# A selective scan on one core: rows of B and C transposed two chunks ahead, y from states over 32 rows, D times x inside the first two products

## What is computed

```python
    dA = jnp.exp(dt[:, :, None, :] * A[None, :, :, None])
    dB = dt[:, :, None, :] * Bt
    def step(h, inp):
        dA_t, dB_t, x_t, C_t = inp
        h = dA_t[:, :, None, :] * h + dB_t[:, :, None, :] * x_t[..., None]
        y_t = jnp.einsum('bhds,bhs->bhd', h, C_t)
        return (h, y_t)
    ...
    return jnp.moveaxis(ys, 0, -1) + D[None, :, None, None] * x
```

## Time and profile before

| | us |
|---|---|
| median of three runs | 1005.8 |
| the profiled execution | 1010.08 |
| its span, first to last instruction | 1008.3 |

### The profile page before, as it was taken

The page is one execution under the profiler, slowest core; times in us unless marked ns, Lnnn a source line. Parts: engine busy times, 40 slices in busy tenths (PEclk is TensorE's granted clock), DMA queues, the critical chain, the costliest instruction groups (busy, mean ns, idle before and its releaser), DMA issues.

```text
span 1008.3 us, 15638 instructions
## 1 busy us (share of the span) xinstructions
PE 916.3 (91%) x4658; PEld 714.5 (71%) x4658; DVE 747.3 (74%) x2003; ACT 534.5 (53%) x1037; POOL 487.7 (48%) x549
## 2 busy tenths in 40 slices
PE   3999899999776787777799999999999999999997
PEld 3887788887454555445678777787777777787776
DVE  5677778564776778666778787788778787788875
ACT  2767677776987998776433332333333332333330
POOL 2145577887788788886544413344034431340000
PEclk8889899999788989778899999999999999999999
DMA  5227765547447444632531401413104131040001
GB/s 171 84 85 215 193 157 171 145 79 234 134 118 171 131 130 124 183 106 86 188 127 43 167 23 39 146 42 144 43 21 166 39 120 70 21 166 21 21 1 42
DMA packets 63690, 110.07 MB, mean 109 GB/s; under 512 B 18539, under 2 KB 44437, under 8 KB 60565
## 3 DMA queue, kind: packets, MB, share of 16 engines
q1 hardware_dynamic: 54388, 90.23, 28.6%
q0 software_dynamic: 7168, 18.03, 6.4%
q10 hardware_dynamic: 2080, 1.19, 0.5%
HBM read 61.51 MB, written 47.92 MB: 109 GB/s over the span
## 4 chain that ended last, share of the span: by engine, by line
PE 66%; DMA 10%; POOL 8%; DVE 6%; issue 4%; SPq 2%; ACT 2%; ACTq 0%; DVEq 0%; POOLq 0%
PE bank L1432 36%; PE bank L1166 8%; PE bank L1341 5%; PE bank L1368 5%; POOL sm L732 4%; DMA bc_scratch<-r 4%; DMA bl<-bc_scratch 3%; PE bank L1396 2%; SPq L460 2%; PE bank L1176 2%; PE bank L1194 2%; PE bank L1380 1%; DMA score_scratch<-score 1%; DVE kbd L1844 1%; DMA xin<-rows_scratch,turn 1%
## 5 line engine op out<-in xcount | busy, mean ns | idle before, releaser
L801 POOL TENSOR_TENSOR ssm<-ssm,rg 128x512 f32<-128x512 f32 x30 | 35.2, 1195 | 255.0 <-DVE ssm L1902 255.0
L1432 PE MATMUL bank<-wexph,xhl 128*128 128x512 f32 x512 | 144.1, 403 | 0.0
L1432 PE MATMUL bank<-wexph,cr 128*128 128x512 f32 x512 | 143.2, 401 | 0.0
L789 POOL DMA_INDIRECT xtm<-y_scratch,idxu x112 | 109.7, 980 | 61.3 <-issue 30.2
L732 POOL TENSOR_TENSOR sm<-sm,rg 128x512 f32<-128x512 f32 x96 | 122.7, 1278 | 29.9 <-DVE rg L1829 17.8
L1829 DVE TENSOR_TENSOR rg<-rg,bank 128x512 f32<-128x512 f32 x112 | 72.4, 679 | 50.5 <-PE bank L1294 43.6
L1432 PEld LDWEIGHTS bank<-wexph,xhl 128*128 128x128 f32 x512 | 93.3, 188 | 22.4 <-DVE xf L2008 1.7
L1432 PEld LDWEIGHTS bank<-wexph,cr 128*128 128x128 f32 x512 | 93.4, 189 | 21.8 <-DVE ysb L2008 1.7
L975 ACT ACTIVATE rg<-dists,aown 128x512 f32<-128x512 f32 x128 | 81.9, 722 | 0.0
L1432 PE MATMUL bank<-wexpl,xhl 128*128 128x512 f32 x256 | 80.7, 396 | 0.0
L1432 PE MATMUL bank<-wexpl,cr 128*128 128x512 f32 x256 | 80.4, 395 | 0.0
(11 more groups left out here) (309 smaller groups left out, 2092.1 us busy)
## 6 DMA issues: line engine op xcount, KB each, us to landing
xin<-in_x SPq DMA_DIRECT2D x16, 1024.0 KB, 5.4
res_gate_scratch<-rg SPq DMA_DIRECT2D x16, 1024.0 KB, 10.6
rg<-res_gate_scratch SPq DMA_DIRECT2D x8, 2048.0 KB
y_scratch<-ysb SPq DMA_DIRECT2D x16, 512.0 KB, 3.7
out<-stage SPq DMA_DIRECT2D x16, 512.0 KB, 2.7
rows_scratch<-stage SPq DMA_DIRECT2D x8, 580.0 KB, 7.2
bc_scratch<-r SPq DMA_DIRECT2D x16, 288.0 KB, 3.9
rows_scratch<-xr SPq DMA_DIRECT2D x6, 580.0 KB, 9.2
```

Source lines behind the costliest of these rows:

```text
L789: pool.indirect_dma_start(out=xtm[:, t, h * P:(h + 1) * P], out_offset=None, in_=y_d[b // GB].rearrange("q p s c -> (q p s) c"), in_offset ...
L1432: last = pe.matmul(bank[4 + i][:, :], x_[:, k, i * P:(i + 1) * P], w[:, 2 * ep * KC + k:2 * ep * KC + k + KC + 1:KC, :], start=(n + k == 0 ...
```

## The change

`rows_of` runs two chunks ahead, at the end of TensorE's body, and `columns` inside the body of its own chunk. `A_BANK` gets four signals in place of two (`rows_out`, `rows_split`, `cols_out`, `cols_copied`, for `a_full` and `a_free`), and `dec` two columns. `rows_high(q+1)` comes first in ScalarE's body and `decays(q+1, 0..2)` at its end, `rows_low(q+1)` first in VectorE's. `states_by_tile` and `hx` are gone: `columns` makes two masked copies of `cw`, even and odd tiles, and `y_of(q, pair)` multiplies 32 rows of one of them by 32 rows of `hs`, for two images of both heads at a time. The add with `dskip` is gone: rows 64 to 127 of `cr[.][0:2]` hold identities, and those of `bl[.][0:2]` D in two parts (`skip_rows`), so that product 0 carries the rounded D on its diagonal and product 1 what the rounding left, both multiplied by exponentials that are 1 there. The diff, cut to its core (renamed waits are left out):

```diff
-        dskip = sb("dskip", [P, SUB])
...
-        hx = [xf[:, i, :].rearrange("p (t c) -> p t c", c=P) for i in range(2)]
-        dec = sb("dec", [P, 1])
+        cwo = [[v[:, i * P:(i + 1) * P] for i in range(4)] for v in (ssm[:, 0, :], xf[:, 1, :])]
+        odd = sb("odd", [P, 2])
+        dec = sb("dec", [P, 2])
...
         def dt_of(c):
+        def odd_columns(c):
+            return cwo[c.q > NT][c.four]
...
             def spread(c):
-                sync.wait_ge(a_free.sem, a_free.at(c.q, 1))
+                sync.wait_ge(rows_split.sem, rows_split.at(c.q, 1))
...
             def add_state(c, s):
-                pool.wait_ge(bc_used[s % 3].sem, bc_used[s % 3].at(c.q, s // 3 + 1))
-                if s == 0:
-                    pool.wait_ge(dskip_ready, 2)
+                if s == 1:
+                    pool.wait_ge(bc_used[0].sem, bc_used[0].at(c.q, 1))
...
-                    pool.wait_ge(summed.sem, summed.at(c.q, s))
-                pool.tensor_tensor(total, bc(dskip[:, :], 1, ST) if s == 0 else total, new, ALU.add).then_inc(
+                    pool.wait_ge(summed.sem, summed.at(c.q, s - 1))
+                pool.wait_ge(bc_used[s % 3].sem, bc_used[s % 3].at(c.q, s // 3 + 1))
+                pool.tensor_tensor(ksum[c.two], ee[:, 0, :] if s == 1 else ksum[c.two], ee[:, s, :], ALU.add).then_inc(
...
             def body(q):
-                for s in range(S - 1):
+                for s in range(1, S - 1):
...
             def rows_high(c):
-                act.wait_ge(a_full.sem, a_full.at(c.q, 1))
-                act.wait_ge(h_ready.sem, h_ready.at(c.q, 0))
-                act.activation(dec[:, :], bank[A_BANK][:, 2 * P:2 * P + 1], ACT.Exp).then_inc(dec_ready.sem, 1)
+                act.wait_ge(rows_out.sem, rows_out.at(c.q, 1))
+                if c.q > 1:
+                    act.wait_ge(h_ready.sem, h_ready.at(c.q - 1, 0))
+                act.activation(dec[:, c.two:c.two + 1], bank[A_BANK][:, 2 * P:2 * P + 1], ACT.Exp).then_inc(dec_ready.sem, 1)
...
             def columns(c):
-                act.wait_ge(a_full.sem, a_full.at(c.q, 2))
-                act.activation(cwt[c.four][:, :], bank[A_BANK][:, 0:P], ACT.Copy).then_inc(a_free.sem, 1)
+                act.wait_ge(cols_out.sem, cols_out.at(c.q, 1))
+                for i, v in enumerate((cwt[c.four][:, :], odd_columns(c))):
+                    act.activation(v, bank[A_BANK][:, 0:P], ACT.Copy, scale=odd[:, i:i + 1]).then_inc(
+                        cols_copied.sem, 1)
...
-                        act.wait_ge(summed.sem, summed.at(c.q - 1, s + 1))
+                        act.wait_ge(summed.sem, summed.at(c.q - 1, max(s, 1)))
...
-            def states_by_tile(c):
-                act.wait_ge(h_ready.sem, h_ready.at(c.q, 2))
-                if c.q > 1:
-                    for h in range(HEADS):
-                        act.wait_ge(y2_full[h].sem, y2_full[h].at(c.q - 2, 1))
-                for t in range(ST):
-                    last = act.activation(hx[c.two][:, t, :], hs[c.four][:, :], ACT.Copy, scale=own_rows[:, t:t + 1])
-                last.then_inc(hx_ready.sem, 1)
...
             def body(q):
-                decays(c, 0, 2)
-                if q + 1 < CHUNKS:
-                    rows_high(Chunk(q + 1))
-                    block_decays(Chunk(q + 1))
+                rows_high(Chunk(q + 1))
+                block_decays(Chunk(q + 1))
...
-                    decays(c, 2, S)
-                    states_by_tile(c)
+                    decays(c, 2, 5)
+                    columns(c)
+                    decays(c, 5, S)
...
-                    decays(c, 4, S)
+                    decays(c, 4, 5)
+                    columns(c)
+                    decays(c, 5, S)
...
-                    states_by_tile(c)
-                if q + 2 < CHUNKS:
-                    up_to_token(Chunk(q + 2))
-                if q + 1 < CHUNKS:
-                    columns(Chunk(q + 1))
+                decays(Chunk(q + 1), 0, 2)
+                up_to_token(Chunk(q + 2))
...
-            columns(Chunk(0))
+            decays(Chunk(0), 0, 2)
...
             def last_chunks():
-                decays(c, 0, 2)
...
-                decays(c, 2, S)
-                states_by_tile(c)
+                decays(c, 2, 5)
+                columns(c)
+                decays(c, 5, S)
...
+                decays(last, 0, 2)
...
+                decays(last, 2, 5)
...
-                decays(last, 0, S)
+                decays(last, 5, S)
...
-                states_by_tile(last)
...
-                y_rows(last, 0)
...
-                y_rows(last, 1)
+                for h in range(HEADS):
+                    y_rows(last, h)
...
-                pe.wait_ge(a_free.sem, a_free.at(c.q, 0))
+                if c.q:
+                    pe.wait_ge(rows_split.sem, rows_split.at(c.q, 0))
+                    pe.wait_ge(dec_ready.sem, dec_ready.at(c.q, 0))
+                if c.q > 1:
+                    pe.wait_ge(cols_copied.sem, cols_copied.at(c.q - 1, 0))
...
             def columns(c):
-                pe.wait_ge(a_free.sem, a_free.at(c.q, 1))
-                pe.transpose(bank[A_BANK][:, 0:P], cw[:, :], ident[:, :]).then_inc(a_full.sem, 1)
+                if c.q + 1 < CHUNKS:
+                    pe.wait_ge(rows_split.sem, rows_split.at(c.q + 1, 1))
+                    pe.wait_ge(dec_ready.sem, dec_ready.at(c.q + 1, 1))
+                pe.wait_ge(w_ready.sem, w_ready.at(c.q, 4))
+                pe.transpose(bank[A_BANK][:, 0:P], cw[:, :], ident[:, :]).then_inc(cols_out.sem, 1)
...
+                    rows_of(Chunk(1))
...
-                    columns(Chunk(0))
...
+                        if c.q == 0:
+                            pe.wait_ge(dskip_ready, 4)
...
-            def y_of(c, i):
-                pe.wait_ge(hx_ready.sem, hx_ready.at(c.q, 1))
+            def y_of(c, pair):
+                pe.wait_ge(h_ready.sem, h_ready.at(c.q, 1))
...
-                pe.wait_ge(y2_used[i].sem, y2_used[i].at(c.q, 0))
-                dst = bank[SY_BANK + i]
-                pe.matmul(dst[:, :], cwt[c.four][:, :], hx[c.two][:, GB * i:GB * (i + 1), :].rearrange("p t c -> p (t c)"),
-                          start=True, stop=False, skip_group_check=True)
-                for b in range(GB):
-                    last = pe.matmul(dst[:, b * P:(b + 1) * P], kbd[:, GB * i + b, :], xr[c.row][:, GB * i + b, 0:P],
-                                     start=False, stop=(b == GB - 1), skip_group_check=True)
-                last.then_inc(y2_full[i].sem, 1)
+                for i in range(HEADS):
+                    dst, rows = bank[SY_BANK + i], slice(PART * (2 * i + pair), PART * (2 * i + pair + 1))
+                    if pair == 0:
+                        pe.wait_ge(y2_used[i].sem, y2_used[i].at(c.q, 0))
+                    else:
+                        pe.wait_ge(y_half.sem, y_half.at(c.q, i + 1))
+                    for b, own in ((2 * pair, cwt[c.four]), (2 * pair + 1, odd_columns(c))):
+                        pe.matmul(dst[:, b * P:(b + 1) * P], own[rows, :], hs[c.four][rows, :],
+                                  start=(b == 0), stop=False, skip_group_check=True)
+                    for b in (2 * pair, 2 * pair + 1):
+                        last = pe.matmul(dst[:, b * P:(b + 1) * P], kbd[:, GB * i + b, :], xr[c.row][:, GB * i + b, 0:P],
+                                         start=False, stop=(b == GB - 1), skip_group_check=True)
+                    last.then_inc((y2_full[i] if pair else y_half).sem, 1)
...
             def body(q):
-                    rows_of(Chunk(q + 1))
...
-                products(c, 1, 4)
+                products(c, 1, 3)
+                columns(c)
+                products(c, 3, 4)
...
+                if q + 2 < CHUNKS:
+                    rows_of(Chunk(q + 2))
...
-                    columns(Chunk(q + 1))
...
+                own.did(dve.tensor_reduce(odd[:, :], own_rows[:, :].rearrange("p (g e) -> p e g", e=2), AX.X, ALU.add))
...
-                part = cr[0][:, :, :] if i == 0 else cr[1][:, 0:S // 2, :]
-                dve.memset(part.bitcast(F32), 0.0).then_inc(cr_zero[i], 1)
+                dve.memset(cr[i][:, 2:S if i == 0 else S // 2, :].bitcast(F32), 0.0).then_inc(cr_zero[i], 1)
+                dve.memset(cr[i][0:SUB, 0:2, :].bitcast(F32), 0.0).then_inc(cr_zero[i], 1)
+                for j in range(2):
+                    dve.tensor_copy(cr[i][SUB:P, j, :].rearrange("p (t n) -> p t n", n=SUB),
+                                    bc(ident[SUB:P, SUB:P], 1, ST)).then_inc(cr_zero[i], 1)
+            def skip_rows():
+                dve.wait_ge(kbd_zero, 3)
+                for v in bl:
+                    for h in range(HEADS):
+                        own.did(dve.tensor_scalar(v[SUB:P, 0, h * SUB:(h + 1) * SUB], ident[SUB:P, SUB:P], dpar[SUB:P, h:h + 1],
+                                          None, ALU.mult))
+                for v in bl:
+                    for h in range(HEADS):
```

(32 more changed lines are left out.)

38 lines of the change are left out of this document (17 added, 21 removed).

## The result

The changed kernel takes 1052.55 us (median of four runs, 1043.15 to 1055.85), the kernel before 1005.52 in the same comparison: ratio **1.047** (95% interval 1.042 to 1.052), slower by 47 us, where 993.4 was forecast and 1005 was the upper end of the range. The profiled execution took 1051.64, with a span of 1049.9 us; TensorE's mean granted clock fell from 0.937 to 0.905.

The account below looks back on a forecast made before the run. A DMA loop bounds the scan's first two thirds, a full GpSimd the last. Gains of 5.0 (nine intervals), 5.7 (four), 1.2 (last) and 0.5 (start) sum to 12.4 us: median 993.4, range 982 to 1005.

Parts of the forecast that it names:

- (3): Chunk's y products: sixteen short instructions make 2.10 us, costing 0.06 more; bounds 1.6 less to 2.1 more; masked copies go.
- (5): TensorE's clock in the scan: mostly 2.4 GHz, one slow half of y in one chunk of six, 0.3 us per chunk.
- (1): Scan's DMA loop: B and C land 7.6 us after `whole_kernel` ends, 10.5 at worst; TensorE's wait for the load goes.
- the load stays last: Rival in the scan: stores at their worst 6.8 us land B and C half a microsecond late; 999 us, chance 10%.
- (2): GpSimd's add with `dskip` goes, 1.44 us per chunk; the four full intervals fall from 14.62 to 13.2 us.
- (4): Next loop, `whole_kernel` through y, ScalarE's copies and exponentials, and the next rows: 12.6 us; GpSimd's loop is 11.5.
- (6): Scan's start and end: 0.5 us gained at the start (1.5 lost to 2 gained), 1.2 in the last whole interval.
- The clock or the switching turns the loop longer: Rival in y's loop: 1.8 us more per chunk, 1011.8 us, 13%; with 0.9 per chunk, 1000 us, 9%.

Follow-up runs that it names:

- grouping: Changed kernel with, in each half of y, both heads' 32-row products first, then both heads' 128-row ones: 1013.49 us, ratio 1.009 to the kernel before.
- the order with y as before: Changed kernel with the earlier y and masked copies, and the next chunk's exponentials ahead of the `y_rows` copies on ScalarE: 998.59 us, ratio 0.999.
- the order: Changed kernel with the next chunk's exponentials and `up_to_token` ahead of the `y_rows` copies on ScalarE: 1030.04 us, ratio 1.029.
- the fill: Idle products in TensorE's two waits, added to the changed kernel (1025.13 us), to exponentials-first with earlier y (1014.09), and to grouped products with exponentials first (996.53).

## Why the prediction was wrong

The step that failed is part (3) with what part (5) built on it: the 32-row products of y were taken to be like the 128-row ones, at a cost of 0.06 us a chunk and with no effect on the clock, for which 0.3 us a chunk was added. Measured, they cost 1.5 us a chunk more than the same products over 128 rows at 2.4 GHz, and with them the clock, once down, stays down to the end of y and beyond: 32.7 us over 13 chunks. With 128 rows in their place the loss is gone (ratio 1.003). The forecast gain doesn't come even so: the first 14 intervals are 193.8 us there, against 182.3 forecast. Slow halves of y and the waits for the loads (see (5) and (1)) are in these 11.5 us; no run takes the two apart.

By intervals the forecast was 14 whole ones of 9 x 12.9 + 4 x 13.2 + 13.37 and a last one as before, 201.95 us in all; measured, 255.35. Those 53.4 us are as much as the miss on the profiled execution (1051.64 - 997.7 = 53.9), in which the earlier start and the longer end cancel. They divide so: the 13 inner intervals at 13.9 instead of 12.9 and 13.2, 9 x 1.0 + 4 x 0.7 = **11.8**; what the seven long ones have above 13.9, **32.7**; the two at the end, 19.68 for 13.37 and 22.29 for 19.68, **8.9**.

- **(1) The DMA loop: right in this kernel, by the help of its long chunks.** TensorE's wait for the loads went from 37.4 us to 1.8 (that of its weight loads from 40.2 to 3.7). The store now takes 4.7 us at the median and 8.6 at most (3.9 and 6.8 before); in chunks of 13.9 us and more the room for it was enough. In shorter ones it was not always: the wait is back with 6.6 us in six pieces with 128 rows, 8.4 in seven with grouping, 15.2 in the order with y as before. So the rival "the load stays last", which had 10%, is hidden here and not refuted.
- **(2) `dskip`: right.** Alone it brings 5 us (0.995, 0.992 to 0.998), where the forecast's term was 5.7. The late intervals went to 12.2 to 13.5, forecast 13.2.
- **(3) The y products: the step that failed.** I took the 32-row instruction at the price of the 128-row `kbd` one, 0.13 us, and put a change of rows at nothing: 2.10 for a pair of quarters. Measured, a pair is 2.56 at full clock, and y 5.5 a chunk where the same products over 128 rows take 4.0. The upper bound (twice, 2.1 a chunk more) held it: +1.5. Between 128-row products the 32-row ones take 0.16 us per instruction against 0.11. The Trainium skill, "TensorE: Matmul & The Clock Gate", section "Why this matters for your kernels", which the prediction had named here, says that a single product over 32 rows takes the same time as one over 128; for these rows that is not so, and the measurement decides. No run has a 32-row product by itself.
- **(4) What is late next: right.** The loop is the one described, 7.2 us of it to within 0.1, and moving the copies off it took 1.5 us from it. With 128 rows the best interval was 12.38, with my sum at 12.6.
- **(5) The clock: right in kind, wrong in size by far.** I gave one chunk in six one slow half, 0.3 us a chunk. The kernel before already has the clock low in 10 places between 267 and 452 us, for less than 7 us each, which the 0.85 of the earlier trace rows sums up and I did not price. With 128 rows one slow half is common and costs 1.6 us or more (13.97 and 15.26 against 12.38). With 32 rows more than half of the chunks are slow in all of y or all but its first quarter, 3.8 to 5.3 us each, 32.7 us in all. The reason I gave against it, that waits of a little over 1 us would not matter where the load's wait was some 4, was read from too few rows. The long chunk follows waits of 1.36 and 2.02 us, and the clock fell inside the second. This is the larger part of the miss, and that the 32 rows keep the clock low was in no part of the sum. The Trainium skill, "TensorE: Matmul & The Clock Gate", section "HAM oscillation — how this bites in real kernels", sets its rule at idle gaps above some 3 us; the chunk above went slow with gaps of 1.36 and 2.02, so the measurement decides here too.
- **(6) The ends: wrong.** The first `whole_kernel` came 3.6 us earlier, not 0.5; but its place varies between 261.8 and 270.8 over the experiments, one profiled execution each, so little rests on it. The last two intervals lost 8.9, as their y is slow too.
- **The rivals.** "The clock or the switching turns the loop longer" is what happened, in both its halves, which I had at 13%, and at 9% for half of its price. That price, 1.8 a chunk for one slow half, gave 1011.8 and left out that y can stay slow to its end, and that the two halves come together: longer quarters at a lower clock.

Over the parts: the early rows and columns are worth nothing or less by themselves (with D, 1.006 against 0.995 without them), since the load's wait makes room for a loop of the same length. With that loop shortened as well, by grouping and the order, the whole reaches 0.989; these ratios are from three chips, and no run tells the share of the early rows in the 0.6 points below 0.995.

## What to carry to other kernels

A product over fewer rows is not free by its sum of columns: cost it with its neighbours, and issue those of different row groups one behind the other, so that they run side by side and the array changes shape less often. When a change takes a long wait out of a loop, add up the loop that is left, and price its TensorE part at 1.2 GHz too wherever waits of 1 to 2 us stay in it. Keep copies that wait for TensorE behind the work that others wait for, since that order alone took 1.5 us from each chunk at 2.4 GHz.

## What the runs showed of the hardware that I had not expected

- Four 32-row instructions of one row group, between 128-row ones, take 0.64 us against 0.44 over 128 rows, and the four 128-row ones ahead of them 0.64 against 0.45. Eight in two row groups, issued together, take 0.65. Whether the first is due to the change of shape, or to the next weights waiting for the same rows, these runs don't tell apart: grouping altered both.
- After a wait of 2.02 us TensorE ran at 1.2 GHz in both kernels compared above; with 128-row products it was back at 2.4 GHz within the same y, with 32-row ones it was not. Over the scan the low clock lasted under 7 us in each of 44 falls without 32-row products, and 13.6 to 20.5 us in each of the six of the changed kernel. Idle products in the waits kept 11 of 13 intervals short, and a chunk after a wait of 2.01 us (the row at 468.75) stayed short without them. The granted clock thus depended on what ran as well as on the waits; what the chip counts is open.
- A higher clock is not always a shorter kernel. Where most chunks were slow, the fill paid (ratio 1.047 to 1.023, clock 0.905 to 0.953); where few were, it raised the clock too, to 0.964 and 0.957, and the kernels became slower (0.999 to 1.011, 0.989 to 0.993).
